# Attention sums inverted through DVE square transpositions, queries moved in two batches, and a new written-out order, in a decoder layer on one core

## The reference, cut to what matters

```
x = x + attn(layernorm(x))            # 16 query heads of 32, one shared key/value head, causal
x = x + smooth_quant_mlp(layernorm(x), fside[b], ctx[b])   # int8 emulated, two products
x = x + ffn(layernorm(x))             # 512 -> 1376 -> 512, LoRA and 8 experts of rank 8, top 2

scores = einsum('bqhd,bkd->bhqk', q, k) * scale          # masked, causal
attn = softmax(scores)
ctx  = einsum('bhqk,bkd->bqhd', attn, v)
```

## Time and profile before

| what | us |
|---|---|
| three timed runs, median | 972.87 |
| three timed runs, lowest and highest | 969.75, 977.21 |
| profiled execution, span from first to last instruction | 968.1 |
| the median above that span | 4.8 |
| PE busy in the span | 918.0 (95%) |
| DVE busy | 616.9 (64%) |
| ACT busy | 316.7 (33%) |
| POOL busy | 313.8 (32%) |
| mean granted TensorE clock | 0.979 of 2.4 GHz |

### The profile page before, as it was taken

One profiled execution on the slowest core, in us unless ns is written; L12 is line 12 of the kernel. 1 busy time (PEld: TensorE's weight loads), 2 busy tenths in 40 slices (PEclk: granted clock), 3 DMA queues, 4 the chain that ended last, 5 costly groups with the idle time before them and its releaser, 6 DMA issues.

```text
span 968.1 us, 13886 instructions
## 1 busy us (share of the span) xinstructions
PE 918.0 (95%) x5333; PEld 678.8 (70%) x5333; DVE 616.9 (64%) x945; ACT 316.7 (33%) x545; POOL 313.8 (32%) x394
## 2 busy tenths in 40 slices
PE   6899999799899999999999999999999999889996
PEld 5775588655468787766778877756778777668885
DVE  3476788578976887766557977754677654432222
ACT  3245521346433234353232243434223331121110
POOL 3556723046831141364200331544014142011110
PEclk9899999799899999999999999999999999999999
DMA  9977545345854733476266433372525446535542
GB/s 313 270 277 293 210 162 130 122 141 205 311 205 123 217 128 132 135 275 247 77 194 176 164 116 143 129 283 104 204 87 177 164 175 214 203 108 188 194 146 93
DMA packets 44967, 175.10 MB, mean 181 GB/s; under 512 B 7197, under 2 KB 10269, under 8 KB 34917
## 3 DMA queue, kind: packets, MB, share of 16 engines
q1 hardware_dynamic: 35780, 114.96, 34.3%
q10 hardware_dynamic: 9120, 59.25, 17.7%
HBM read 127.46 MB, written 33.75 MB: 167 GB/s over the span
## 4 chain that ended last, share of the span: by engine, by line
PE 75%; DMA 7%; DVE 4%; SPq 4%; POOL 4%; issue 3%; ACT 2%; POOLq 0%; DVEq 0%; ACTq 0%
PE ring L1000 12%; PE ring L1001 11%; PE ring L1002 11%; PE slots L1073 4%; PE ring L1236 4%; PE av L1104 4%; PE ring L997 3%; PE slots L1090 3%; PE den L1104 3%; PE slots L1000 3%; PE slots L1002 3%; PE slots L1001 3%; SPq L605 3%; DMA qst<-negm_hl 3%; PE slots L1173 2%
## 5 line engine op out<-in xcount | busy, mean ns | idle before, releaser
L775 POOL TENSOR_TENSOR hd_l<-hd,hd_h 128x512 fp32r<-128x512 f32 x44 | 57.4, 1305 | 293.7 <-ACT hd_h L967 293.6
L1000 PE MATMUL ring<-xT_h,gu 128*128 128x512 f32 x352 | 143.0, 406 | 2.0 <-DMA gu<-gu_parts 1.9
L1002 PE MATMUL ring<-xT_h,gu 128*128 128x512 f32 x352 | 138.3, 393 | 0.0
L1001 PE MATMUL ring<-xT_l,gu 128*128 128x512 f32 x352 | 138.1, 392 | 0.0
L1354 DVE TENSOR_REDUCE negm<-slots 128x1 f32<-128x384 f32 (+3 forms) x176 | 105.9, 636 | 35.2 <-PE slots L1073 34.7
L869 ACT ACTIVATE probs<-slots 128x512 f32<-128x512 f32 (+1 forms) x176 | 90.4, 555 | 95.4 <-PE slots L1090 94.9
L742 POOL TENSOR_SCALAR_AFFINE_SELECT probs<-probs 128x128 f32<-128x128 f32 (+2 forms) x176 | 65.5, 386 | 100.3 <-ACT probs L869 99.8
L1000 PEld LDWEIGHTS ring<-xT_h,gu 128*128 128x128 f32 x352 | 66.5, 189 | 20.8 <-issue 8.5
L1599 DVE TENSOR_TENSOR total<-ring,total 128x512 f32<-128x512 f32 x64 | 44.0, 688 | 51.8 <-PE ring L1002 51.6
L1002 PEld LDWEIGHTS ring<-xT_h,gu 128*128 128x128 f32 x352 | 66.5, 189 | 14.8
L1001 PEld LDWEIGHTS ring<-xT_l,gu 128*128 128x128 f32 x352 | 66.8, 190 | 11.8
(11 more groups left out here) (196 smaller groups left out, 1839.3 us busy)
## 6 DMA issues: line engine op xcount, KB each, us to landing
gu<-gu_parts ACTq DMA_DIRECT2D x42, 1280.0 KB, 5.5
dn<-dn_parts SPq DMA_DIRECT2D x12, 1728.0 KB, 7.4
gu_parts<-gu SPq DMA_DIRECT2D x11, 1280.0 KB, 5.8
qst<-qT_h SPq DMA_DIRECT2D x128, 64.0 KB, 2.8
raw_gu<-gu SPq DMA_DIRECT2D x11, 640.0 KB, 7.3
dn_parts<-dn SPq DMA_DIRECT2D x11, 576.0 KB, 7.6
dn<-dn_parts SPq DMA_DIRECT2D x4, 1152.0 KB, 5.2
x_in<-x SPq DMA_DIRECT2D x8, 512.0 KB, 6.3
```

The costliest lines, as they stand in the source:

```text
L775: pool.tensor_tensor(hd_l[:, i, :], hd[:, i, :], hd_h[:, i, :].bitcast(F32), ALU.subtract).then_inc(hd_lo.sem, 1)
L1000: pe.matmul(out_, w_hi_, m_hi_, start=start, stop=False, skip_group_check=True)
L1001: pe.matmul(out_, w_hi_, m_lo_, start=False, stop=False, skip_group_check=True)
L1002: return pe.matmul(out_, w_lo_, m_hi_, start=False, stop=stop, skip_group_check=True)
```

## The change

Four things change.

1. Sums. ACT's copy of `den` (L876) goes. DVE transposes `den` from PSUM into `rden` in squares of 32x32 (128x512), copies `av` as before, takes the reciprocal of one column of each square (128x16, into the new tile `rsum`), and transposes `rsum`, each value repeated 32 times, back into `rden` (128x512). `context` only multiplies. Two waits of DVE on its own results come in.
2. Queries. SP moves the identity row of all 16 heads in one DMA of 32 KB, then tile 0 by 8 DMAs of 64 KB as before, and tiles 1 to 3 together by 8 DMAs of 192 KB once tile 3 is there. ACT likewise: 4 DMAs for tile 0 and 4 of 192 KB for the rest. SP issues 17 and ACT 8 per batch. Maxima of groups 1 to 3 wait for the one semaphore of the rest.
3. Order. `TURNS` is new.
4. Fills. The new `TURNS` has no digits.

The diff, with the inner lines of the two strings left out:

```
@@ -278,26 +278,23 @@
 
 
 TURNS = (
-    "1111A111AA1A11111111AAA1A11A111A1A11111A111AAAWAA1111111111111111XXX1WW111111111XXXX1111111XXX1111111111AXXXXX"
...
-    "FFFFFFFFFFFFFFFFFFFFFFFFFFFFFFFFFFFFFFFFFFFFFFFFFFFFFFFFFFFFFFFFFFFFFFFFFFFFFFFFFFFF")
+    "AAAAAAAAAAAAAAAAAXXXWXXXXXWAXXXAXXWXXXWXXXXXXXXAXXAAAAAXAWAXAWAWWAXAXAXAAXXWXAWAXXXXAAAAAAAAAAAAAXAWAAAWAXAAAA"
...
+    "FFFFFFFFFFFFFFFFFFFFFFFFFFFFFFFFFFFFFFFFFFFFFFFFFFFFFFFFFFFF")
 
 
 def in_order():
@@ -383,6 +380,7 @@
         negm_hl = sb("negm_hl", [HD + 4 * TT, 4, P], F32R)
         negm_h, negm_l = negm_hl[0:4 * TT, :, :], negm_hl[HD:HD + 4 * TT, :, :]
         rden, cx = sb("rden", [P, T]), sb("cx", [P, 2, T])
+        rsum = sb("rsum", [P, T // HD])
         vT = rden
 
         heads_at = region(HEADS * T * 4)
@@ -461,12 +459,13 @@
         kv_ps, kv_act, kv_lo = sig("kv_ps"), sig("kv_act", 3), sig("kv_lo")
         q_ps, q_hi, q_lo = sig("q_ps", KT), sig("q_hi", KT), sig("q_lo", KT)
         v_ps, v_ready = sig("v_ps"), sig("v_ready")
-        q_moved, m_moved = [sig(f"q_moved{i}", 16 * 13) for i in range(KT)], [sig(f"m_moved{i}", 32) for i in range(4)]
+        q_moved, m_moved = [sig(f"q_moved{i}", 16 * (13 - i)) for i in range(2)], [sig(f"m_moved{i}", 32) for i in range(4)]
         s_ps, s_max = sig("s_ps", 4 * MG), sig("s_max", 4 * MG)
         m_ps, m_hi, m_lo = sig("m_ps", 4), sig("m_hi", 4), sig("m_lo", 4)
         t_ps, p_exp, p_ready = (sig(name, SCORES_TO[-1]) for name in ("t_ps", "p_exp", "p_ready"))
         pv_done = sig("pv_done", 16)
-        av_out, den_out, rden_ready = sig("av_out", 4), sig("den_out", 4), sig("rden_ready", 8)
+        av_out, den_out, rden_ready = sig("av_out", 4), sig("den_out", 4), sig("rden_ready", 4)
+        rsum_ready = sig("rsum_ready", 4)
         cx_ready, cx_hi, cx_lo = sig("cx_ready", 8), sig("cx_hi", 8), sig("cx_lo", 8)
         wo_loaded, o_ps, x1_ready = sig("wo_loaded", 16), sig("o_ps", 2), sig("x1_ready", 2)
 
@@ -495,6 +494,15 @@
         ad_ps, ad_added = sig("ad_ps", len(SEGMENTS)), sig("ad_added", len(SEGMENTS))
         out_ps, out_added = sig("out_ps", TT * len(SEGMENTS)), sig("out_added", TT * len(SEGMENTS))
         ff_link = sig("ff_link", FF_LINKS)
+
+        def tiles_moved(e):
+
+            return slice(0, 1) if e == 0 else slice(1, KT)
+
+        def moved_heads(row, e, j):
+
+            heads = qst[row:row + HD, :, :].bitcast(F32).rearrange("p (e j) t -> p e j t", j=4)
+            return heads[:, tiles_moved(e), j, :]
 
         def product_of(b, n):
 
@@ -594,16 +602,19 @@
                     sp.dma_start(wqkv_l[:, :, :].bitcast(F32), parts[:, 1]).then_inc(wqkv_loaded.sem, 16)
 
             def q(b, e):
-                if b == 0 and e < 2:
-                    sp.wait_ge(w_lo.sem, KT)
-                elif b and e == 0:
-                    sp.wait_ge(o_ps.sem, o_ps.at(b - 1, 2))
-                sp.dma_start(qst[KROWS:MROW, 4 * e:4 * e + 4, :].bitcast(F32), mask_r[0:4 * TT, 0, :].bitcast(F32)).then_inc(q_moved[e].sem, 16)
+                if e == 0:
+                    if b == 0:
+                        sp.wait_ge(w_lo.sem, KT)
+                    else:
+                        sp.wait_ge(o_ps.sem, o_ps.at(b - 1, 2))
+                    sp.dma_start(qst[KROWS:MROW, :, :].bitcast(F32), mask_r[0:HEADS * TT, 0, :].bitcast(F32)).then_inc(q_moved[0].sem, 16)
+                if e not in (0, KT - 1):
+                    return
                 sp.wait_ge(q_hi.sem, q_hi.at(b, e + 1))
                 for row in (0, 2 * HD):
                     for j in range(4):
-                        sp.dma_start(qst[row:row + HD, 4 * e + j, :].bitcast(F32), qT_h[HD * j:HD * j + HD, e, :].bitcast(F32))\
-                          .then_inc(q_moved[e].sem, 16)
+                        sp.dma_start(moved_heads(row, e, j), qT_h[HD * j:HD * j + HD, tiles_moved(e), :].bitcast(F32))\
+                          .then_inc(q_moved[min(e, 1)].sem, 16)
 
             def rows_(b, g):
                 sp.wait_ge(m_hi.sem, m_hi.at(b, g + 1))
@@ -834,22 +845,22 @@
                 if b and e == 0:
                     act.wait_ge(pv_done.sem, pv_done.at(b - 1, 16))
                 act.activation(qT_h[:, e, :], ps[:, 0, :], ACT.Identity, bias=bq_sb[:, e:e + 1]).then_inc(q_hi.sem, 1)
-                if e:
-                    low_rows(b, e - 1)
+                if e == 1:
+                    low_rows(b, 0)
 
             def v_(b):
                 low_rows(b, KT - 1)
 
             def low_rows(b, e):
 
-                if b == 0 and e < 2:
+                if b == 0:
                     act.wait_ge(w_lo.sem, KT)
-                elif b and e == 0:
+                elif e == 0:
                     act.wait_ge(o_ps.sem, o_ps.at(b - 1, 2))
                 act.wait_ge(q_lo.sem, q_lo.at(b, e + 1))
                 for j in range(4):
-                    act.dma_start(qst[HD:2 * HD, 4 * e + j, :].bitcast(F32), qT_l[HD * j:HD * j + HD, e, :].bitcast(F32))\
-                       .then_inc(q_moved[e].sem, 16)
+                    act.dma_start(moved_heads(HD, e, j), qT_l[HD * j:HD * j + HD, tiles_moved(e), :].bitcast(F32))\
+                       .then_inc(q_moved[min(e, 1)].sem, 16)
 
             def rows_(b, g):
                 act.wait_ge(m_ps.sem, m_ps.at(b, g + 1))
@@ -864,16 +875,10 @@
                 if step >= 2:
                     act.wait_ge(pv_done.sem, pv_done.at(b, step - 1))
                 elif step == 0 and unit == 0:
-                    for e in range(KT):
-                        act.wait_ge(q_moved[e].sem, q_moved[e].at(b, q_moved[e].per))
+                    for moved in q_moved:
+                        act.wait_ge(moved.sem, moved.at(b, moved.per))
                 act.activation(probs[:, at:at + heads, 0:n], slot("scores", b, step, unit)[:, 0, 0:heads * n].rearrange("p (h n) -> p h n", n=n),
                                ACT.Exp, scale=SCALE).then_inc(p_exp.sem, 1)
-
-            def sums(b, g):
-                act.wait_ge(pv_done.sem, pv_done.at(b, 4 * g + 4))
-                if g:
-                    act.wait_ge(cx_ready.sem, cx_ready.at(b, 2 * g))
-                act.activation(rden[:, :], den[:, :], ACT.Copy).then_inc(den_out.sem, 1)
 
             def split_context(b, g, hf):
                 cols = slice(T // 2 * hf, T // 2 * (hf + 1))
@@ -976,7 +981,7 @@
                 act.activation(y_g[:, :], y[:, :], ACT.Copy).then_inc(y_hi.sem, 1)
 
             steps = {"prep_small": prep_small, "prep_wo": prep_wo, "prep_gu": prep_gu, "prep_dn": prep_dn, "turn1": turn1, "kv": kv,
-                     "q": q, "v": v_, "rows": rows_, "scores": scores, "sums": sums, "split_context": split_context, "tanh": tanh,
+                     "q": q, "v": v_, "rows": rows_, "scores": scores, "split_context": split_context, "tanh": tanh,
                      "s_rows": s_rows_, "round_a": round_a, "round_w": round_w, "copy_a": copy_a, "copy_w": copy_w, "w_row": w_row,
                      "turn3": turn3, "low_in": low_in, "router": router, "logits": logits, "w_turn": w_turn, "y": y_, "gate": gate,
                      "hid": hid_, "yd": yd}
@@ -1062,7 +1067,8 @@
                     if b == 0:
                         pe.wait_ge(consts_ready.sem, 6)
                 if i == 0:
-                    pe.wait_ge(q_moved[g].sem, q_moved[g].at(b, q_moved[g].per))
+                    for moved in q_moved[min(g, 1):min(g, 1) + 1]:
+                        pe.wait_ge(moved.sem, moved.at(b, moved.per))
                 qt, h0, heads = MAX_GROUPS[i]
                 n = (qt + 1) * P
                 ps = in_slots.claim(pe, ("max", b, g, i), s_max, s_max.at(b, MG * g + i + 1))
@@ -1365,13 +1371,17 @@
                     dve.wait_ge(cx_lo.sem, cx_lo.at(b, 2 * g - 2))
                 elif b:
                     dve.wait_ge(cx_lo.sem, cx_lo.at(b - 1, 8))
+                dve.transpose(rden[:, :], den[:, :]).then_inc(den_out.sem, 1)
                 dve.tensor_copy(cx[:, g % 2, :], av[:, :]).then_inc(av_out.sem, 1)
+                dve.wait_ge(den_out.sem, den_out.at(b, g + 1))
+                squares = rden[:, :].rearrange("p (c r) -> p c r", r=HD)
+                dve.reciprocal(rsum[:, :], squares[:, :, 0]).then_inc(rsum_ready.sem, 1)
+                dve.wait_ge(rsum_ready.sem, rsum_ready.at(b, g + 1))
+                dve.transpose(squares, rsum[:, :].unsqueeze(2).to_broadcast([P, T // HD, HD])).then_inc(rden_ready.sem, 1)
 
             def context(b, g, hf):
                 cols = slice(T // 2 * hf, T // 2 * (hf + 1))
-                dve.wait_ge(den_out.sem, den_out.at(b, g + 1))
-                dve.reciprocal(rden[:, cols], rden[:, cols]).then_inc(rden_ready.sem, 1)
-                dve.wait_ge(rden_ready.sem, rden_ready.at(b, 2 * g + 1 + hf))
+                dve.wait_ge(rden_ready.sem, rden_ready.at(b, g + 1))
                 dve.wait_ge(av_out.sem, av_out.at(b, g + 1))
```

101 lines of the change are left out of this document (54 added, 47 removed).

## The result

The kernel after takes 1001.7 us (four runs, 999.1 to 1007.4) against 971.3 for the kernel before (four runs): ratio 1.029, interval 1.024 to 1.035. The forecast was 945.5. The change is 3% slower, outside the range.

The account below looks back on a forecast made before the run. The prediction saw an early part (35 to 257 us) waiting for chains and a late part of some 96% work. Its terms summed to -27.4 us, from 972.87 (span 968.1 plus 4.8) to 945.5; range 924 to 967.

Parts of the forecast that it names:

- signs named beforehand for "wrong": Clock below 0.9 where the span grows, transposition over 1.2 us, query waits at group 1's maxima, or unchanged batch 1 distance.
- Start: 0 to 35 us: without fills the projections start at 1.2 GHz and query tile 0's copy comes later; +2.5 us.
- Batch 0's first scores: Fewer maxima ahead of the first scores and fewer DMAs for SP to issue bring them earlier; -6 us.
- Rest of batch 0: Batch 0's attention to 120 us: cheaper sums and two preparation tiles moved out; -6 us.
- Sums: Each group's sum costs DVE 2.4 instead of 4.18 us; only batch 1's three before 257 us count, -5.4 us.
- Queries in batch 1: Fewer SP and ACT issues and earlier rows: `kv` to first scores 35 us instead of 41.5; -6.5 us.
- Queries in batches 2 and 3: Feed-forward work hides the query issues there, so fewer issues gain nothing.
- Layer 0: 180 to 257 us: roundings -3, batch 1's last maxima rows issued earlier -4, sums -5.4; -12.4 us in all.
- Clock: Sparse early stretches without fills: a tenth of the 154 us of work meets the lower clock; +5 us.
- cold PE: Rival: without fills the clock falls and early work on the path doubles, 991.5 us; chance 0.1.
- After 257: From 257 us on: fewer fills -0.5, POOL's bias step no longer held by its DMA -3.5; -4 us.
- The median above the span: The median of the runs was taken to stay 4.8 us above the profiled span.

Follow-up runs that it names:

- e18: Kernel before with new sums and old query moves; from the end of batch 0's attention on, the new order without fills; 978.7 us, 1.004.
- e13: As e18, but with the weight preparation behind the same steps as in the old order; 998.5 us, 1.022.
- e9: Kernel before with new sums and old query moves; new order without fills only up to the end of batch 0's attention; 992.0 us, 1.023.
- e1: Kernel before with its own order, sums and queries, all 354 fill steps taken out; 980.8 us, 1.008.
- e5: Kernel after with the old query moves (new order, new sums, no fills); 992.8 us, 1.018 against the kernel before.
- e6: Kernel after with 611 fill matmuls put into its own PE waits, up to 300 us; 1016.4 us, 1.044 against the kernel before.
- e2: Kernel after with the 354 old fill steps put back behind the same PE steps; 1006.5 us, 1.032 against the kernel before.
- e4: Kernel before with only the new sums; 976.0 us, 1.002.
- e11: Kernel before with the new sums and only ACT's four low-part query DMAs of tiles 2 and 3 joined; 977.6 us, 1.004.
- e12: e4 with one step moved: the weight save of tile 6 stands behind batch 1's first maxima rows; 966.8 us, 0.991 against the kernel before.
- e3: Kernel after in the old order with its fills (new sums, new query moves); 1004.8 us, 1.030 against the kernel before.
- e17: As e18, but 17 steps moved from between `turn_a` and batch 0's first products to behind them; 986.8 us, 1.012.
- e15: e12 with every second fill step between batch 1's first maxima and first scores left out; 971.3 us, 0.995 against the kernel before.

## Why the prediction was wrong, step by step

Two of the signs named beforehand for "wrong" came: a clock below 0.9 in windows where the span grew (0.66 and 0.68), and PE waiting for query transfers at group 1's maxima. `turn3` of batch 0 came 19.8 us later, not 25 to 30 earlier.

**Start: the number right, by luck.** +2.5 forecast, +2.5 measured. But the first maxima start at 33.9 to 40.5 us in the runs that begin like the kernel before, with all its fills (e18 and e13 are the ends), and at 32.7 to 37.7 without fills (e9, e1, the kernel after, e5). No cost of the missing fills is shown there.

**Batch 0's first scores: right in kind, half in size.** -6 forecast, -2.8 measured. In e6, where fills kept the clock, the way from first maxima to first scores takes 18.4 us against 23.9 before and 21.1 in the kernel after. So the order may be worth 5.5 and the lost clock took 2.7 of it back; single traces of the new order spread, though (e5 21.1, e9 23.2, and e2, with the old fills, 24.6).

**Rest of batch 0: wrong sign.** -6 forecast, +15.3 measured. "Two preparation tiles move out" was true, and I counted it as a relief for waiting scores. The same steps without fills took 75.8, 72.9 and 80.3 us (after, e5, e9); the old order took 66.0 without fills (e1) and 60.3 to 65.0 with them. By e1, at most 5.5 us of the 15.3 are the missing fills; in e6, at a clock of 0.95, the stretch is as long as in the kernel after, with 28.5 us of fills in it. What in the order costs the rest was not taken apart.

**Sums: the size right, the worth wrong.** The transpositions took what was forecast. The tile `rden` of the kernel after (min/median/max ns):

```profile
L1374 DVE STREAM_TRANSPOSE rden<-den x16: 682/716/718, 89.8 to 723.6; 128x512 f32<-128x512 f32 x16
L1378 DVE RECIPROCAL rsum<-rden x16: 226/232/235, 91.0 to 724.8; 128x16 f32<-128x16 f32 x16
L1380 DVE STREAM_TRANSPOSE rden<-rsum x16: 711/712/714, 91.3 to 725.1; 128x512 f32<-128x512 f32 x16
```

0.72 + 0.23 + 0.71 us and the copy against 4.18: about -29 us of DVE in all, as forecast, of which 24.4 show in e4's busy time and 16.8 in the kernel after, where the normalising of `x_in` alone takes 16.9 us instead of 11.2. The forecast put 5.4 us of it on the path since DVE was "nearly the bound" in 180 to 257. e4 shows none (1.002): 61.5 busy of 77 us is an average, which doesn't tell who is waited for last. The prediction's price for transpositions of 1.4 us each, a gain of 1.2 us, should read 3 x (4.18 - 3.84) = 1.0, and half of 0.688 is 0.34, not its bound of 0.5; neither changes the forecast. The Trainium skill, page "Vector Engine (DVE) Microarchitecture Reference", section "The reshape front-end and per-opcode configuration", gives one element per cycle per lane, and the runs agree: a transposition costs what the 0.69 us copy of the shape costs, also when it reads one column 32 times.

**Queries in batch 1: the sum right, the terms not.** Forecast 35 us from `kv` to first scores, measured 35.1 against 41.7 before. But 4.1 of the 6.6 us come from a transfer that took 5.95 us to land before and 1.87 after, and which I took as given ("some 5 to land"). It was late because the weight save stood ahead of it on SP; after, SP issues the rows at 183.40 and the save at 184.64:

```profile
183.40 1.20 SPq L623 DMA_DIRECT2D qst<-negm_hl  x2
184.64 0.58 SPq L557 DMA_DIRECT2D gu_parts<-gu  x1
```

The row transfer lands in 1.87 us:

```profile
184.00 1.87 DMA qst<-negm_hl
```

I credited the issues saved on SP and ACT. e11 shows that four of ACT's are worth nothing, and e12 that the old moves reach 36.0 us with one step moved.

**Queries in batches 2 and 3: the step that failed most plainly.** "In batches 2 and 3 feed-forward work hides the issues: nothing." The issues were hidden, the landing wasn't. The bound that I worked out for batch 1 (tiles 1 to 3 land last) held there: its wait was 0.9 us. I didn't ask it of batches 2 and 3, where the old trace had group 1's maxima 25 us behind `kv` and the same sum gave a landing at 25 to 28; it came at 33.5. Cost in the new order: 9 us by e5, of which batch 2 shows 8.4 (49.0 against 40.6 from `kv` to first scores). In the old order it is 29 us by e3 against e4, and there batch 0, of which I didn't ask it either, has a share: 12.4 us more from first maxima to first scores.

**Layer 0: wrong sign.** -12.4 forecast, +13.8 measured. By the windows under e6, PE idled for 6.6 us before and 11.8 after (+5.2), the fills went (-13.2), and the rest of PE's busy time rose from 57.4 to 79.2 (+21.8): some 6.6 of that is work moved into the stretch, by e2, and the other 15 I put down to the lower clock, an estimate. I took this stretch's length for a chain of waits that each edit shortens by its own term (rounding behind scores, rows ahead of `x2_save`). PE work, fills and clock traded places instead. Neither moving the preparation back (e13) nor bringing the first product forward by 5 to 9 us (e17) shortened it. Which order of these steps would is open.

**Clock: +5 forecast, too small, and not to be had back.** In the old order the fills are worth 8 us (e1). In the new one the lower clock costs, by the estimate above, some 15 us in the layer stretch alone, of which the fills that are gone pay 13. Putting fills back gives nothing (e2: +5, e6: +15). The likely reason is that they stand where PE has work that is late; no run isolates it. The rival "cold PE" named the mechanism of this part; its 991 is near e5's 993, the kernel after without the query transfers' cost, but it took the fills for free and the new order for a gain, so that the two agree by luck. The Trainium skill, page "TensorE: Matmul & The Clock Gate", section "What's actually happening", calls the throttled state the default that activity releases. The traces agree: 0.66 without fills where 0.94 was granted with them. The price is another matter: e15 shows where it is due, in dense work right behind a gap.

**After 257: wrong.** -4 forecast, +17.7 measured, of it some 8 at batch 2's queries, 3.8 net around batch 3's start (+10.9, -7.1) and the rest in smaller steps. POOL's waits for the DMA ahead of a bias step fell from four (27.4 us) to one in batch 0 (17.5), as forecast, and no gain shows for it. ACT's busy time, the reciprocals and the two runs of query issues came as listed under "what would show it right"; each was true, and none bought time.

**The median above the span: luck of the draw.** I kept 4.8 us between the profiled span and the median. In the kernel after the median is 3.9 us below the span, as the slowest run was the profiled one. It is a scatter between executions and no term of a sum.

## What to carry to other kernels

Ask of a transfer when its last byte lands and who asks for it first, once for every stage that uses it, not only for the stage that you study. A small transfer on the path should be issued ahead of the large ones that nobody waits for yet: one step moved gave 1%. An order that was searched for is one object: its single swaps can each be argued well while the whole is some 17 us slower, so test an order in halves before you take it apart in words. Fills and the lower clock are two prices for the same gaps: compare time, not clock. And before profiles are compared step by step, see where the profiled execution lies among its runs: here 7 of 37.5 us were that.
